# Cross-attention on one core: the first of eight batches rebuilt

## What is computed

```python
q = jnp.einsum('bcn,dc->bnd', x1, Wq) + bq
k = jnp.einsum('bcn,dc->bdn', x2, Wk) + bk[:, None]
v = jnp.einsum('bcn,dc->bdn', x2, Wv) + bv[:, None]
attn = jax.nn.softmax(jnp.einsum('bnd,bdm->bnm', q, k), axis=2)
attn_out = jnp.einsum('bcm,bnm->bcn', v, attn)
return attn_out + x1
```

## Time and profile before

| | us |
|---|---|
| median of 3 runs | 664.24 |
| lowest, highest | 662.16, 664.27 |
| the profiled execution's own time | 664.22 |
| its span, first to last instruction | 662.4 |
| PE busy in it | 649.9 |
| DVE, ACT, POOL busy | 469.9, 282.5, 122.1 |

### The profile page before, as it was taken

One profiled execution on the slowest core, in us unless ns is written; L12 is line 12 of the kernel. 1 busy time (PEld: TensorE's weight loads), 2 busy tenths in 40 slices (PEclk: granted clock), 3 DMA queues, 4 the chain that ended last, 5 costly groups with the idle time before them and its releaser, 6 DMA issues.

```text
span 662.4 us, 8349 instructions
## 1 busy us (share of the span) xinstructions
PE 649.9 (98%) x2848; PEld 533.2 (80%) x2848; DVE 469.9 (71%) x510; ACT 282.5 (43%) x367; POOL 122.1 (18%) x51
## 2 busy tenths in 40 slices
PE   5999999999999999999999999999999999999997
PEld 3877788888888888888888888888888888888886
DVE  4889758687487685785777866869668696587541
ACT  5665513546235453364433733237523456135120
POOL 0302300143003230033200540006300053002100
PEclk9999999999999999999999999999999999999999
DMA  8800632873439633596325862177632865325352
GB/s 318 300 32 2 175 113 77 233 234 105 127 95 276 192 96 100 130 306 170 96 89 134 295 174 95 63 171 265 166 95 68 219 247 131 121 74 137 84 162 73
DMA packets 94874, 100.04 MB, mean 151 GB/s; under 512 B 8336, under 2 KB 69776, under 8 KB 94864
## 3 DMA queue, kind: packets, MB, share of 16 engines
q1 hardware_dynamic: 94864, 99.91, 50.8%
...
## 4 chain that ended last, share of the span: by engine, by line
PE 95%; DVE 3%; DMA 1%; ACT 0%; issue 0%; SPq 0%; DVEq 0%
PE acc_ps L726 51%; PE acc_ps L695 26%; PE s_ps L665 9%; PE s_ps L673 4%; PE s_ps L674 4%; DVE probs L489 1%; DMA stage<-in_ctx_dram 1%; PE s_ps L786 1%; DVE blocks L498 1%; DVE negmax L482 1%; DVE xs_lo L447 0%; ACT probs L334 0%; ACT xs_hi L299 0%; DVE o_sb L515 0%; DVE vt_lo L447 0%
## 5 line engine op out<-in xcount | busy, mean ns | idle before, releaser
L726 PE MATMUL acc_ps<-pt_lo,vt_hi 128*128 128x512 f32 x512 | 199.3, 389 | 0.0
L726 PE MATMUL acc_ps<-pt_hi,vt_lo 128*128 128x512 f32 x512 | 199.3, 389 | 0.0
L726 PE MATMUL acc_ps<-pt_hi,vt_hi 128*128 128x512 f32 x512 | 199.3, 389 | 0.0
L334 ACT ACTIVATE probs<-s_ps,negmax 128x1024 f32<-128x1024 f32 x64 | 71.4, 1116 | 128.5 <-DVE negmax L482 128.5
L726 PEld LDWEIGHTS acc_ps<-pt_hi,vt_hi 128*128 128x128 f32 x512 | 96.1, 188 | 20.5 <-DVE pt_lo L447 0.3
L726 PEld LDWEIGHTS acc_ps<-pt_lo,vt_hi 128*128 128x128 f32 x512 | 96.1, 188 | 20.1
L726 PEld LDWEIGHTS acc_ps<-pt_hi,vt_lo 128*128 128x128 f32 x512 | 96.1, 188 | 20.0
L268 POOL TENSOR_TENSOR pt_lo<-pt_raw,pt_hi 128x1024 fp32r<-128x1024 f32 x14 | 41.0, 2949 | 356.3 <-ACT pt_hi L299 356.3
L695 PE MATMUL acc_ps<-wv_hi,xs_hi 128*128 128x512 f32 x256 | 99.8, 390 | 0.0
L695 PE MATMUL acc_ps<-wv_hi,xs_lo 128*128 128x512 f32 x256 | 99.7, 389 | 0.0
L695 PE MATMUL acc_ps<-wv_lo,xs_hi 128*128 128x512 f32 x256 | 99.6, 389 | 0.0
...
## 6 DMA issues: line engine op xcount, KB each, us to landing
...
```

Source lines behind the costliest of these rows:

```text
L334: nc.scalar.activation(probs[:, t % 2, :], s_ps[:, t % 2, :, :].rearrange("p a n -> p (a n)"), ACT.Exp, bias=negmax[:, t:t + 1], accum_out ...
L726: mm = nc.tensor.matmul(acc_ps[:, c % BANKS, :], v[:, m, cols], p[:, m, :], start=(m == 0 and v is vt_hi and p is pt_hi), stop=(m == MT - ...
```

## The change

Only the first batch is changed, and the first execution of `batch`, which is written out ahead of the loop; the loop has one batch fewer. Later batches keep their code.

- **Loads.** The first tile of `x2` comes in two halves of 256 KB, and each tile of `x2` is followed by its tile of `Wv`. `Wk` and `Wq` are laid out on the host so that a partition reads 1 KB in one piece.
- **PE order.** V groups 0 to 3 are accumulated side by side in the four banks, behind each tile of `x2`, together with k. q goes to slot 1 of `s_ps`, k to slot 0; q's sum, high and low part are made in halves of 512 columns.
- **Banks.** V groups 4 to 7 take banks 0, 1, 0, 1; the transposes of scores 0 to 3 go to banks 2 and 3 (the last to 0 and 1) of `acc_ps`, not to `s_ps`.
- **Normalising.** In the first batch POOL multiplies scores 0 to 5 by the reciprocal, and ACT scores 6 and 7; DVE only takes the reciprocals. Scores 0 to 3 have four buffers (`probs0`, in the memory of `blocks`).
- **Scores 6 and 7** are made inside the outputs of `h` = 0, before step (0, 6) and before step (1, 0).
- **Zeros.** Two matmuls on a zeroed buffer stand at the very start of PE.

```diff
+V_BANK0 = (0, 1, 2, 3, 0, 1, 0, 1)
+T_BANK0 = (2, 2, 2, 0)
...
+            sp.dma_start(stage2[:, 0, 0:NH], x2_d[0, 0:P, 0:NH]).then_inc(s_head, 16)
+            weight(0)
+            sp.dma_start(wk_raw, wk_d.rearrange("p (k d) -> p k d", d=D)).then_inc(s_wk, 16)
+            sp.dma_start(stage2[:, 0, NH:N], x2_d[0, 0:P, NH:N]).then_inc(s_in2[0], 16)
+            for k in range(1, KT):
                 load_x2(0, k)
...
+                weight(k)
+            load_x1(0, 0)
...
+            def first_normalise(p, t):
+                pool.wait_ge(s_inv, t + 1)
+                nc.gpsimd.tensor_scalar(p, p, inv[:, t:t + 1], None, ALU.mult).then_inc(s_norm, 1)
...
-                exp(b, 7)
+                if first:
+                    round_x1(nb, 0)
+                    round_x1(nb, 1)
+                    exp(b, 6)
+                    round_x1(nb, 2)
+                    first_normalise(6)
+                    exp(b, 7)
+                    round_x1(nb, 3)
+                    first_normalise(7)
...
+            pe.wait_ge(s_warm, 1)
+            for i in range(2):
+                nc.tensor.matmul(s_ps[:, 1, i, :], probs[:, 0, 0:P], probs[:, 0, 0:NH], start=True, stop=True)
...
+            for k in (1, 2):
+                pe.wait_ge(s_x2hi, k + 1)
+                first_k(k, 0)
+                pe.wait_ge(s_wvhi, k + 1)
+                first_v_term(k, xs_hi, wv_hi)
                 pe.wait_ge((s_x2lo_e, s_x2lo_o)[k % 2], k // 2 + 1)
...
+                first_k(k, 1)
+                first_v_term(k, xs_lo, wv_hi)
                 pe.wait_ge(s_wvlo, k + 1)
...
+                first_v_term(k, xs_hi, wv_lo)
...
+            first_v_group(5, part=1)
+            scores_next(0, 2)
+            first_v_group(6, part=0)
             pe.wait_ge(s_ident, 1)
             first_turn(0)
+            scores_next(0, 3)
+            first_v_group(6, part=1)
             first_turn(1)
...
+            first_v_group(7)
             first_turn(2)
             first_turn(3)
...
+            pe.wait_ge(s_qlo, 1)
+            scores_next(0, 4)
+            scores_next(0, 5)
+            pe.wait_ge(s_plo, 2)
+            pe.wait_ge(s_plo_odd, 2)
+            batch(0, False, first=True)
+            with pe.Fori(1, B - 1) as b:
```

More of the change, by code:

```diff
@@ L411, in _ @@
+            copy(wk_s[:, :, 0:D], wk_raw).then_inc(s_wkhi, 1)
+            first_x2_hi(0)
+            for k in range(1, KT):
+                first_x2_hi(k)
+                weight_hi(k)
+            first_x1_hi(0)
             act.wait_ge(s_wq, 16)
             copy(wq_s[:, :, 0:D], wq_raw).then_inc(s_wqhi, 1)
-            for k in range(KT):
-                if k == KT - 1:
-                    v_hi(0, 0)
-                act.wait_ge(s_in1[k], 16)
-                copy(x0_hi[:, k, :], stage1[:, k, :]).then_inc(s_x1hi, 1)
@@ new lines, in _ @@
+            dve.wait_ge(s_headhi, 1)
+            sub(xs_lo[:, 0, 0:NH], stage2[:, 0, 0:NH], xs_hi[:, 0, 0:NH]).then_inc(s_headlo, 1)
+            weight_lo(0)
+            dve.wait_ge(s_wkhi, 1)
+            sub(wk_s[:, :, D:2 * D], wk_raw, wk_s[:, :, 0:D]).then_inc(s_wklo, 1)
+            first_x2_lo(0)
+            for k in range(1, KT):
+                first_x2_lo(k)
+                weight_lo(k)
+            first_x1_lo(1)
+            first_k_sum()
+            first_v_lo(0)
+            first_x1_lo(3)
@@ L752, in v_phase, with batch @@
                         scores_next(b, NT + (1, 2, 4, 5).index(m))
-            def batch(b, last):
+            def batch(b, last, first=False):
                 nb = b + 1
@@ L758, in batch @@
                     for m in range(MT):
+                        if first and (c, m) == (0, 6):
+                            scores_next(0, 6)
+                        if first and (c, m) == (1, 0):
+                            scores_next(0, 7)
                         if (c, m) == (2, 0) and not last:
@@ L788, in first_turn, with first_k @@
                 mm.then_inc(s_blk, 1)
-            def first_scores(t):
-                pe.wait_ge((s_plo, s_plo_odd)[t % 2], t // 2)
-                scores(t)
-            pe.wait_ge(s_wklo, 1)
-            for k in range(KT):
+            def first_k(k, part):
+                for h in range(HALVES):
+                    mm = nc.tensor.matmul(s_ps[:, 0, h, :], wk_s[:, k, :],
+                                          (xs_hi, xs_lo)[part][:, k, h * NH:(h + 1) * NH],
+                                          start=(k == 0 and part == 0), stop=(k == KT - 1 and part == 1))
+                return mm
@@ new lines, in first_v_term, with first_v_last @@
+            def first_v_term(k, x, w):
+                for m in range(BANKS):
+                    nc.tensor.matmul(acc_ps[:, m, :], x[:, k, m * P:(m + 1) * P], w[:, k, :],
+                                     start=(k == 0 and x is xs_hi and w is wv_hi), stop=False)
+            def first_v_last(m):
+                k = KT - 1
+                for x, w in ((xs_hi, wv_hi), (xs_lo, wv_hi), (xs_hi, wv_lo)):
+                    mm = nc.tensor.matmul(acc_ps[:, m, :], x[:, k, m * P:(m + 1) * P], w[:, k, :],
+                                          start=False, stop=(w is wv_lo))
+                mm.then_inc(s_v, 1)
@@ new lines, in first_v_group @@
+            def first_v_group(m, part=None):
+                if part != 1:
+                    pe.wait_ge(s_acc, BANKS + (1, 2, 5, 6)[m - 4])
+                for k in range(KT // 2 if part == 1 else 0, KT // 2 if part == 0 else KT):
+                    for x, w in ((xs_hi, wv_hi), (xs_hi, wv_lo), (xs_lo, wv_hi)):
+                        mm = nc.tensor.matmul(acc_ps[:, V_BANK0[m], :], x[:, k, m * P:(m + 1) * P], w[:, k, :],
+                                              start=(k == 0 and x is xs_hi and w is wv_hi),
+                                              stop=(k == KT - 1 and x is xs_lo))
+                if part != 0:
+                    mm.then_inc(s_v, 1)
@@ new lines, in first_q @@
+            def first_q(k):
+                pe.wait_ge((s_x1lo_e, s_x1lo_o)[k % 2], k // 2 + 1)
+                for h in range(HALVES):
+                    for part, x in enumerate((x0_hi, x0_lo)):
+                        cols = x[:, k, h * NH:(h + 1) * NH].rearrange("p (i t r) -> p t i r", i=NQ, t=NT)
+                        mm = nc.tensor.matmul(s_ps[:, 1, h, :], wq_s[:, k, :], cols,
+                                              start=(k == 0 and part == 0), stop=(k == KT - 1 and part == 1))
+                    if k == KT - 1:
+                        mm.then_inc((s_qa, s_q)[h], 1)
@@ new lines, in _ @@
+            for m in range(BANKS):
+                first_v_last(m)
+            pe.wait_ge(s_wqlo, 1)
+            first_q(0)
+            first_q(1)
+            first_v_group(4, part=0)
+            first_q(2)
+            first_q(3)
+            first_v_group(4, part=1)
+            first_v_group(5, part=0)
+            pe.wait_ge(s_klo, 2)
+            pe.wait_ge(s_qlo_a, 1)
+            scores(0)
+            pe.wait_ge(s_qsum, 1)
+            scores(1)
+            first_v_group(5, part=1)
@@ L833, in _ @@
-            v_group(0, 7, part=1)
-            scores_next(0, 6)
-            scores_next(0, 7)
-            with pe.Fori(0, B - 1) as b:
+            pe.wait_ge(s_qlo, 1)
[3 more added lines that the diff above has]
+            pe.wait_ge(s_plo_odd, 2)
+            batch(0, False, first=True)
+            with pe.Fori(1, B - 1) as b:
                 batch(b, False)
```

269 lines of the change are left out of this document (169 added, 100 removed).

## The result

The changed kernel takes **667.74 us** (median of five, 666.89 to 668.14), the kernel before 663.68 beside it: ratio 1.0061, 95% interval 1.0044 to 1.0077. A second set of five, run with the last experiments, gave 667.45 (667.37 to 668.64) and 1.0059 (1.0045 to 1.0073). The forecast was 662.0: the change makes the kernel 4 us slower, and the time lies outside the range. The profiled execution took 666.91, its span is 664.7, so 2.2 us lie outside it, 1.8 before. The kernel before scatters by itself: 72 executions beside the experiments lie between 661.94 and 664.89, all with a mean granted clock of 0.999 or 1.000, and what moves them was not looked for.

The account below looks back on a forecast made before the run. PE was taken as the bound, busy 649.9 of 662.4 us, with the time following turn(7)'s end. turn(7) 2.2 us earlier gave 664.2 - 2.2 = 662.0 us; range 659.4 to 664.7.

Parts of the forecast that it names:

- The start: Start of PE: first V matmul at about 4.8 instead of 6.97, clock rising at 9.9, k done at 19.0.
- four matmuls followed by a gap: Kernel before, PE from 6.97: spacing stayed 0.45 after them, so the two matmuls on zeros were given no effect.
- the rival of an early clock: Start of PE: high clock by 4.8, k done 2.4 us earlier, time 659.6, or 660.8 for half; chance 0.22.
- P: Time of one 128x1024 product on POOL, normalising first-batch scores; taken as 1.0 us.
- The bounds of 0.75 and 3.34: Limits for one POOL product: DVE's 0.75 for the same product, POOL's 3.34 for a subtraction with DVE in its way.
- the rival's P - 1.9: First transpose: its wait if a POOL product takes over 1.9 us; 0.5 at 2.41, 1.4 at 3.34.
- 2P - 3.9: turn(5): its slide from needing two POOL products in a row; 0.9 at 2.41, 2.8 at 3.34.
- The rival: POOL's products are slow and delay the first transpose and turn(5): 663.4 at 2.41 us, 666.2 at 3.34; chance 0.09.
- break-even of 2.7: POOL product time in us at which the forecast gain is gone (0.8 + 1.5).
- the 15.06 of the chain beside it: From turn(7)'s end through DMA, ACT and DVE to the outputs of half 1: 15.06 us, untouched by the change.
- PE's outputs 5 us earlier: First batch: PE starts the outputs 5 us earlier, at 49.4, but is stopped again below.
- The time follows the end of turn(7): First batch: a microsecond won counts only if it reaches turn(7)'s end, forecast at 63.95 instead of 66.19.

Follow-up runs that it names:

- the experiment: The changed kernel with the products of scores 0 to 5 all back on DVE; measured 661.96 us, ratio to the kernel before 0.9983.

## Why the prediction was wrong, step by step

**The start: right in time, wrong in clock.** The first V matmul came at 4.97 (4.8 taken). The zeros, to which I gave no effect, kept PE at work until 5.02, and the V matmuls were fast at once; without them k's last matmul started at 18.72 and was done near 19.1, as forecast. I had reasoned from four matmuls followed by a gap; here the zeros lead into the real work without one. They are in plain `float32` and fill the time well: two matmuls stand in the trace as four pieces and take 3.58. The last of k started at 17.72 and was done near 18.1, 0.9 ahead of my 19.0 (the rival of an early clock had 2.4). Of that 0.6 was left at scores 0 (29.61 for 30.2), since ACT, POOL and DVE set that path.

**P: the step that failed.** "For one input I take the nearest row" gave 1.0 us by scaling a select of 128 columns. It is 2.85. The bounds of 0.75 and 3.34 held it, but the value came from a row of another operation and an eighth of the size: 0.8 ns a column, where the product needs 2.4 to 2.5. The Trainium skill, GPSIMD Engine Reference, section 4.1, calls one input roughly line rate; the copy agrees (1.04), the product doesn't (2.77 with a constant, 2.85 with a number per partition), and the measurement decides. Its first advice, VectorE for elementwise work, agrees with the experiments.

**What P did.** The first transpose came at 37.13 instead of 36.3, the fourth at 47.41 instead of 46.1, maximum 4 at 50.73 instead of 49.4: 1.3, where the rival's P - 1.9 = 0.95 had seen only the first transpose; the pair at 41.68 holds up the fourth as well. turn(5) ended at 60.43 instead of 57.2 (another 1.9; 2P - 3.9 = 1.8). Together 3.2 at turn(7), against 2.75 by the rival's formula and 3.16 by the experiment. The rival was the right mechanism, and 0.09 was too little for it. Its break-even of 2.7 was not tested; with its slope of 3 us for each us of P, from the 3.2 measured at 2.85, turn(7) would be back at 66.19 at P = 2.5 (an estimate).

**The fall behind the wait: not priced at all.** The rival at P = 2.85 gives 662.0 + 2.75 = 664.75; measured are 667.5 to 667.7. 0.45 of the difference is turn(7), later than the formula has it, mostly by the fourth transpose, which makes 665.2. Without the fall 665.6 was measured; the 0.4 above that sum is the time outside the span, 2.2 for 1.8, a term that I had taken as fixed. The rest, 1.9 to 2.1, went with the fall of TensorE's clock, 1.5 of it seen between turn(7) and half 1: I had counted the 60 matmuls behind the low part at 0.23 each, 14.9 us, "as long" as the 15.06 of the chain beside it, and so with no slack. After a wait of 3.5 eight of them ran at 0.43, which makes 16.5. I had used the spacing at the start of the kernel as evidence, and not asked whether a later wait could bring it back. The forecast had put PE's outputs 5 us earlier, so the wait was in the plan.

**What held.** The time follows the end of turn(7), until PE itself becomes the path: by the fall of the clock, as in the changed kernel, or since turn(7) is early enough (the kernels with the scores earlier). ACT's product took 1.15 (1.05 taken). With the products on DVE at 0.76, turn(7) ended at 63.99 for 63.95, and the median was 661.96 for 662.0. The closeness of the median is in part luck: five of the twelve executions had a fall of the clock, which the forecast did not have, and with two more the median would be near 663. The loop was unchanged: 581.0 to 581.5 in all kernels.
